# An expert tile's third products are made before, not behind, the next tile's second products

## The reference

```
gate_scores = softmax(x @ Wg); top 2 of 8 experts, their scores made to sum to 1
gate  = x @ W11[e]          # 256 -> 512, "first products"
value = x @ W12[e]          # 256 -> 512, "second products"
fused = gate * sigmoid(gate) * value
expert_out = fused @ W2[e]  # 512 -> 256, "third products"
out = sum over the two chosen experts of score * expert_out
x = x + 0.5 * out           # before and after the mixer
```

## Time and profile before

| | |
|---|---|
| median of 3 runs | 966.09 us (965.93 to 966.66) |
| the profiled execution | 961.58 us, its span 959.8 us |
| PE busy, share of the span | 898.3 us, 94% |
| DVE, POOL, ACT busy | 61%, 60%, 41% |
| chain that ended last, by engine | PE 81%, DVE 7%, DMA 4%, ACT 2% |
| the same, largest lines | L1492 (g and v) 40%, L1515 (D) 21%, L1501 (H) 6%, L1484 (T) 3% |
| pass 0 of the experts | 60 to 415 us |
| pass 1 of the experts | 598 us to the end |

### The profile page before, as it was taken

How to read it: one execution, slowest core, us unless ns; L and a number is a source line. 1 busy time by engine, 2 the same in 40 slices (tenths; PEclk the granted TensorE clock), 3 DMA queues, 4 the chain that set the end, 5 groups by cost and what they waited for, 6 DMA issues and landing times.

```text
span 959.8 us, 19122 instructions
## 1 busy us (share of the span) xinstructions
PE 898.3 (94%) x5429; PEld 773.5 (81%) x5430; DVE 583.2 (61%) x1386; ACT 391.8 (41%) x768; POOL 575.4 (60%) x616
## 2 busy tenths in 40 slices
PE   7869999999999999968999986999999999999994
PEld 7748888888888888846876874788888888888883
DVE  4886565665666655568745987555555555555551
ACT  3834344343443433316635775333333333333331
POOL 4836566655666665427605663577777777777762
PEclk9979999999999999979999987999999999999997
DMA  9743625526345182168202646743434433333321
GB/s 322 260 156 120 206 74 188 184 79 208 111 152 203 58 276 88 39 202 275 67 3 85 198 155 212 256 96 69 77 55 77 77 54 77 53 74 54 55 45 23
DMA packets 83745, 121.51 MB, mean 127 GB/s; under 512 B 12944, under 2 KB 62480, under 8 KB 83696
## 3 DMA queue, kind: packets, MB, share of 16 engines
q1 hardware_dynamic: 44032, 56.57, 17.9%
q0 software_dynamic: 25088, 37.59, 17.9%
q10 hardware_dynamic: 14576, 26.75, 8.2%
HBM read 73.62 MB, written 47.25 MB: 126 GB/s over the span
## 4 chain that ended last, share of the span: by engine, by line
PE 81%; DVE 7%; DMA 4%; ACT 2%; issue 2%; POOL 1%; ACTq 1%; POOLq 0%; SPq 0%; DVEq 0%
PE bank L1492 40%; PE bank L1515 21%; PE bank L1501 6%; PE bank L1614 3%; PE bank L1484 3%; PE bank L1430 3%; DMA w_lo<-w_lo_rows 2%; PE bank L1675 2%; PE bank L1631 1%; DVE states L1353 1%; DMA out_rows<-yb,idx_i 1%; PE bank L1665 1%; PE bank L1602 1%; DVE work L1361 1%; ACT work L829 1%
## 5 line engine op out<-in xcount | busy, mean ns | idle before, releaser
L1197 DVE TENSOR_TENSOR sg<-sg,bank 128x512 f32<-128x512 f32 x142 | 97.7, 688 | 281.8 <-ACT sg L758 281.8
L1492 PE MATMUL bank<-w_hi,xt_hi 128*128 x568 | 235.5, 415 | 7.0 <-DVE xt_lo L1186 6.1
L1492 PE MATMUL bank<-w_hi,xt_lo 128*128 x568 | 223.4, 393 | 0.0
L1492 PE MATMUL bank<-w_lo,xt_hi 128*128 x568 | 223.3, 393 | 0.0
L750 ACT ACTIVATE yb<-bank,gates_in 128x256 f32<-128x256 f32 x142 | 67.5, 475 | 313.3 <-PE bank L1515 273.2
L555 POOL DMA_INDIRECT xg<-xn_rows,idx_i x142 | 139.9, 986 | 62.4 <-issue 41.7
L559 POOL DMA_INDIRECT gates_in<-gate_rows,idx_g x142 | 135.6, 955 | 52.0 <-issue 42.7
L1515 PE MATMUL bank<-w_hi,ft_hi 128*128 x568 | 160.1, 282 | 2.2 <-ACT yb L750 2.2
L1515 PE MATMUL bank<-w_hi,ft_lo 128*128 x568 | 160.3, 282 | 0.0
L1515 PE MATMUL bank<-w_lo,ft_hi 128*128 x568 | 160.3, 282 | 0.0
L569 POOL DMA_INDIRECT out_rows<-yb,idx_i x71 | 114.7, 1616 | 59.9 <-ACT yb L750 45.0
(11 more groups left out here) (290 smaller groups left out, 1296.4 us busy)
## 6 DMA issues: line engine op xcount, KB each, us to landing
w_lo<-w_lo_rows SPq DMA_DIRECT2D x32, 512.0 KB, 4.5
w_lo_rows<-w_lo ACTq DMA_DIRECT2D x16, 512.0 KB
xn_rows<-work SPq DMA_DIRECT2D x14, 512.0 KB, 3.2
x_all<-x SPq DMA_DIRECT2D x8, 512.0 KB, 10.3
w_lo_rows<-in_sb ACTq DMA_DIRECT2D x16, 256.0 KB, 2.4
gate<-x SPq DMA_DIRECT2D x16, 256.0 KB, 7.3
seq<-y_rows SPq DMA_DIRECT2D x8, 512.0 KB, 5.1
seq<-w ACTq DMA_DIRECT2D x7, 512.0 KB, 4.4
```

The lines of the kernel that those rows point to most:

```text
L1197: nc.vector.tensor_tensor(sg[p], sg[p], ps_g[p][:], ALU.mult).then_inc(f_step, 1)
L1492: last = nc.tensor.matmul(dst[p][:], xt[p][:, c, :], of(w), start=(c == 0 and n == 0), stop=(c == DC - 1 and n == len(parts) - 1))
```

## The change

In `tile`, the D block of tile t-2 is issued before the v block of tile t. A tile's order on PE was g, T, H, v, D and becomes g, T, H, D, v. Nothing is added or removed; waits and semaphores move with their blocks. Both passes use the same function. The other engines' programs are not touched.

```diff
                     if early > 0:
                         hidden_in(t - 1, 1 - p)
-                    up(p, w12_hi, w12_lo, ps_v, e, v_done)
                     if early > 1:
                         down(t - 2, p, e_before)
+                    up(p, w12_hi, w12_lo, ps_v, e, v_done)
```

## The result

| | us | ratio to before, 95% interval |
|---|---|---|
| before, 10 runs beside it | 967.45 (965.93 to 969.6) | |
| changed kernel, 10 runs | 971.82 (968.82 to 972.81) | 1.0041 [1.0031, 1.0051] |
| forecast | 964.6 (962.6 to 967.6) | |

The change made the kernel slower, by 4.4 us. Its profiled execution took 971.92 us (span 970.2), close to its median. Two kernels of the table further down each have one execution far off the rest (2266 us in before_third, 1297 us in gates_first_before_2), and the ratios leave these two out.

What follows compares the result with a forecast made beforehand. PE's matmuls bound the kernel, 4.85 us per tile. Stalls -1.98, end of pass 0 +0.46, end of pass 1 -1.39 and seams +1.4 sum to -1.5, from 966.09 to 964.6 us; range 962.6 to 967.6.

Steps and rivals of the forecast that it cites:

- seams: Block boundaries in every tile: D behind H's transposes takes 0.01 us more, +1.4 us over 138 tiles.
- end of pass 0: Last tiles of pass 0: H(70) waits uncovered for fu(70), delaying D(69), D(70) and the last scatter; +0.46 us.
- end of pass 1: Last three scatters of pass 1: earlier yb(68) moves their chain forward; -1.39 us, bounded by -1.4 and -0.7.
- The rival of the mixer's pace: v and g back to back run at the mixer's 2.80 to 2.81, 0.05 us per tile: 970.1 us; chance 0.13.
- the one of free seams: Neighbouring blocks on PE hardly matter, so seams cost 0: sum -2.9, 963.2 us; chance 0.34.
- After the change yb comes 1.38 earlier and the stores with it ... the stall goes. Worth: -1.98: Pass 0: ACT's sigmoid is late by only 0.58, within slack, so PE's waits for xt_lo vanish; -1.98 us.
- smaller ones, which have the same cause: Smaller stalls of pass 0, put down to ACT issuing loads behind yb, vanish too; included in -1.98 us.
- D(69) follows at once: End of pass 0: D(69) starts at 410.60 right behind H(70) at 410.16; +0.46 us, bounded by +0.4 and +0.7.
- In hand: 0.45 ... I cost this at nothing: Every tile: after v, fu lets H start at 1.16 while it is due at 1.61; no stall, cost 0.
- fu holds H: H waits for fu in tiles; 0.1 us stall per tile gives 978.6 us; chance 0.05 together with the unknown.

Runs made afterwards that it cites:

- before_third: The unchanged kernel run again, in a group without late signals: 961.13 us, ratio 0.9993 to the kernel before at 961.54.
- gates_first_before_2: Old order on PE, with POOL gathering the gates of tile t+1 ahead of the rows of tile t+4: 961.6 us, ratio 0.9995 to the kernel before.
- the two befores of that group: The unchanged kernel measured twice in the group where the changed kernel took 981.49 us: 972.8 us, and 972.13 us when run again.
- after_third: The changed kernel run again without edits, in a group without late signals: 964.35 us, ratio 1.0025 to the kernel before at 961.54.
- pass1_new: The changed kernel with the new order in pass 1 only, pass 0 in the old order: 978.18 us, ratio 1.0043 to the kernel before.
- pass0_new: The changed kernel with the new order in pass 0 only, pass 1 in the old order: 978.02 us, ratio 1.0051 to the kernel before.
- the second pair with gates first: Old and new order on PE, both with POOL gathering gates ahead of rows, beside before at 961.54: 961.6 and 963.24 us.
- after_again: The changed kernel run again without edits, in a group with late signals: 981.49 us, ratio 1.0102 to the kernel before at 972.8.

## Why the prediction was wrong

**The sum.** Forecast -1.5. Without late signals it is: seams +1.3, stalls about 0, end of pass 0 +1.4, end of pass 1 -0.3 to -0.6, together +2.3; measured in such a group +2.8 (964.35 and 961.54). With them it was +9.4 and +8.7 against the two befores of that group. The first comparison's +4.4 lies between, with 87 late signals and a clock that fell; how it divides between these two I can't say, because before was traced there only in its quick execution.

**Seams: right.** Taken 0.01 us per tile; the periods are 4.850 and 4.860 in the undisturbed traces, and v with g is 2.77. The rival of the mixer's pace was wrong, the one of free seams too. That rival's gap by the number of columns, from the Trainium skill ("TensorE: Matmul & The Clock Gate", Back-to-back issue gap), had said 0. The Trainium skill gives that gap for a matmul by itself, not for a stream of weight loads and matmuls, as it runs here. The trace has 0.01 us a tile that depends on the neighbour.

**"After the change yb comes 1.38 earlier and the stores with it ... the stall goes. Worth: -1.98": the failed step.** The mechanism worked. In after_third, at the tile of the earlier trace rows, ACT's work stands so:

```profile
100.42 0.48 ACT L750 ACTIVATE yb<-bank,gates_in 128x256 f32<-128x256 f32 x1 [0.84 <-PE bank L1515]
...
102.99 0.38 PE L1484 MATMUL bank<-ident,xg 128*128 128x128 f32 x2
103.19 0.60 ACT L758 ACTIVATE sg<-bank 128x512 f32<-128x512 f32 x1 [2.29 <-PE bank L1492]
...
106.65 0.19 PEld L1492 LDWEIGHTS bank<-w_hi,xt_hi 128*128 128x128 f32 x1 [0.44 <-issue]
```

The sigmoid is 0.20 behind T, on time. But the next g stops for 0.27 all the same, before a weight load, for a reason that the profile does not name ("issue"), and stops of 0.1 to 0.3 come once or twice in every eight tiles. And there was less to gain than I took: my 1.98 was one execution's. before_third has 1.0 in the same stretch (321.13 us apart, the period taken as 4.85), after_third 1.9. The term is 0 or a little above, not -1.98.

The step also took the cause of the small stalls wrong. Between tiles 3 and 69 of pass 0 the trace of before has one wait of PE for xt_lo, the 0.90 of the earlier trace rows, and before_third has none. The tile of that wait is 1.16 us longer than a period; the other 0.8 us are five stops of 0.1 to 0.3 in which PE waits for no engine, so ACT's earlier yb could not take them away. The "smaller ones, which have the same cause" were of another kind.

Where signals are on time, three terms make nearly the whole miss: +2.0 here, +0.9 in the next step, and 0.9 of the end of pass 1 that was not gained, 3.8 us of the 4.3 between -1.5 and +2.8.

**"D(69) follows at once": wrong, by 0.9.** I had +0.46 and a bound of +0.7; it is +1.37. H(70), behind a wait, took 0.63 in the chain, not 0.44; D(69) then began 0.55 late ("issue": PE loads the expert of the tile from memory just there, L1520, and before this lay under yb's wait); and D behind a gap took 1.82, not the 1.59 that I gave it. That the gap could lower the clock I did not think of: in two of the traces with the new end (17.70 and 17.53 us) it did, in six (15.5) it did not. It costs another 2.1 us. What decides between the two is open.

**The end of pass 1.** Forecast -1.39 with a bound of -0.7; measured -0.3 to -0.8 between traces of the two orders in a group. Two pairs lie outside: 0.05 earlier only (pass1_new against pass0_new), and 2.0 earlier (the second pair with gates first), where the old order took 19.58 and its other traces 17.9 to 18.1. The first scatter moved as worked out; yb(69) did not, for the same gap between H(70) and D(69).

**"In hand: 0.45 ... I cost this at nothing".** The arithmetic holds: 0.38 measured, and in the undisturbed group H waits in no ordinary tile. What failed is what it was measured against. The 0.04 us from a matmul's end to its reader was read from a trace in which no signal of PE was late, of an execution that took 961.58 where the timed runs took 966. I wrote that difference down and carried the terms over it. In other executions the signal of a block comes 0.25 us to over 3 us late in one case out of four to seven. Before the change v was followed by D, 1.4 us more of cover for fu; afterwards only T and a part of g are left. I gave "fu holds H" 0.05 and 978.6 us; it is in the main what happened where before was at 972.8 (981.49; of the 6.6 us between the spans 4.8 are H's waits for fu).

The forecast chance of slower was 0.16. Both mechanisms that spoke for slower, an uncovered chain at a pass's end and a thin cover for fu, stood in my own text with their prices, each one at its most favourable end.

## What to carry to other kernels

Slack read from one trace is slack of that execution: where the profiled run is quicker than the timed ones, take the difference as stalls that the trace doesn't show, and ask whose cover they would eat. If a block that feeds another engine is moved to the last place, that makes that engine's answer uncovered once at each end of the loop, and its cover thin inside it; work out the ends with everything that a restart costs (wait, register load, slower first matmuls, perhaps the clock). A stall that one execution shows is worth at most its smallest size over several. And before small stalls are put down to the cause of the largest, look whether the engine waits for anything in them.

## What the runs showed of the hardware

- Signals of PE (not of ACT or DVE) can be recorded 0.25 to 3.7 us after the matmul that gives them, several let go together (128.11 to 128.22 in after_again). It was seen only in some groups, in 87 to 155 of some 600 recorded. Without the gathers of 128 rows of 4 bytes in each tile six were left in each of two traces, all but one of the twelve at the four gathers that begin each pass; in the groups at 961 no signal was late with all gathers in place. Late signals cost before some 10 us. The same chip gave 972.8 us in one group and 961.3 in a later one. What decides it is open.
- The same schedule with PE idle for 1.3 us of 4 was followed by a granted clock of 0.57 in one execution and of 1.00 in another. D's twelve matmuls then took 2.83 to 2.95 or 1.82.
- D, twelve matmuls, takes 1.43 behind busy PE and 1.81 to 1.82 behind an idle one.
